# Causal maxima in a decoder kernel: two units to a turn on TensorE, scores in two strips of rows and two banks

## What is computed

```python
scores = jnp.einsum('bhqd,bhkd->bhqk', q, k) * SCALE
mask = _window_mask(N, N)
scores = jnp.where(mask[None, None], NEG_INF, scores)
attn = jax.nn.softmax(scores, axis=-1)
out = jnp.einsum('bhqk,bhkd->bhqd', attn, v)
```

## Time and profile before

| | us |
|---|---|
| three runs, median | 1609.12 |
| three runs, lowest and highest | 1601.79, 1609.81 |
| profiled execution | 1603.94 |
| its span | 1602.2 |
| PE busy | 1361.3 |
| DVE busy | 1332.5 |
| ACT busy | 1037.2 |
| mean granted clock of PE | 0.939 |

### The profile page before, as it was taken

The page is one execution under the profiler, slowest core; times in us unless marked ns, Lnnn a source line. Parts: engine busy times, 40 slices in busy tenths (PEclk is TensorE's granted clock), DMA queues, the critical chain, the costliest instruction groups (busy, mean ns, idle before and its releaser), DMA issues.

```text
span 1602.2 us, 32850 instructions
## 1 busy us (share of the span) xinstructions
PE 1361.3 (85%) x13068; PEld 745.7 (47%) x13068; DVE 1332.5 (83%) x1965; ACT 1037.2 (65%) x1884; POOL 428.2 (27%) x495
## 2 busy tenths in 40 slices
PE   3778878879899999898978767879999998999986
PEld 2454535344445453444443333446555555555643
DVE  6988989979879888887798899888788888978743
ACT  3244365465673865765695769886899788989431
POOL 1432141132240422321331240241222313122310
PEclk9697989799999999999999988889999999999988
DMA  6313122200201111002120003011020211101020
GB/s 223 93 54 93 34 68 68 74 15 1 75 15 41 36 41 42 21 22 54 63 89 28 1 1 132 20 41 44 2 71 13 59 39 33 41 5 44 2 81 27
DMA packets 54201, 76.24 MB, mean 48 GB/s; under 512 B 8480, under 2 KB 23840, under 8 KB 53536
## 3 DMA queue, kind: packets, MB, share of 16 engines
q1 hardware_dynamic: 54048, 74.14, 16.2%
HBM read 38.98 MB, written 9.44 MB: 30 GB/s over the span
## 4 chain that ended last, share of the span: by engine, by line
PE 47%; DVE 29%; ACT 10%; issue 7%; POOL 4%; DMA 1%; SPq 1%; ACTq 0%; DVEq 0%; POOLq 0%
PE bank L200 16%; DVE mix_NM L1079 4%; PE bank L1178 4%; PE bank L534 3%; DVE ssm_HS L1537 2%; PE bank L542 2%; PE bank L522 2%; PE bank L992 2%; PE bank L1204 2%; PE bank L557 2%; DVE ffn_m L1133 2%; PE bank L977 2%; POOL attn_P L737 2%; PE bank L495 1%; DVE ffn_Z L1142 1%
## 5 line engine op out<-in xcount | busy, mean ns | idle before, releaser
L1052 ACT ACTIVATE mix_P<-bank 128x512 f32<-128x512 f32 x256 | 142.3, 604 | 50.6 <-PE bank L977 50.2
L1079 DVE TENSOR_REDUCE mix_NM<-bank 128x2 f32<-128x512 f32 x256 | 162.8, 682 | 11.2 <-PE bank L952 10.4
L737 POOL TENSOR_SCALAR_AFFINE_SELECT cross_P<-cross_P 128x256 f32<-128x256 f32 x128 | 90.5, 717 | 272.9 <-ACT cross_P L642 272.4
L1296 POOL TENSOR_TENSOR ffn_room<-ffn_room 128x512 f32<-128x512 f32 x64 | 89.9, 1406 | 263.9 <-ACT ffn_room L1235 167.0
L1537 DVE TENSOR_TENSOR_SCAN ssm_HS<-ssm_DA,ssm_DD 128x1024 f32<-128x1024 f32 x64 | 150.3, 2348 | 10.1 <-ACT ssm_DD L1488 5.5
L737 POOL TENSOR_SCALAR_AFFINE_SELECT attn_P<-attn_P 128x256 f32<-128x256 f32 x128 | 89.6, 713 | 243.7 <-ACT attn_P L642 243.7
L1485 ACT ACTIVATE ssm_DA<-ssm_Z,A_T 128x255 f32<-128x255 f32 x256 | 110.9, 498 | 3.1 <-DVE ssm_HS L1537 2.7
L642 ACT ACTIVATE attn_P<-bank 128x384 f32<-128x384 f32 x128 | 63.8, 498 | 63.1 <-PE bank L523 62.7
L642 ACT ACTIVATE cross_P<-bank 128x384 f32<-128x384 f32 x128 | 62.6, 489 | 50.9 <-PE bank L523 50.5
L1543 DVE TENSOR_TENSOR ssm_HS<-ssm_HS,ssm_CS 128x1024 f32<-128x1024 f32 x64 | 82.0, 1281 | 0.9
L1460 ACT ACTIVATE ssm_Z<-bank 128x512 f32<-128x512 f32 x128 | 72.2, 599 | 13.4 <-PE bank L1374 12.8
(11 more groups left out here) (410 smaller groups left out, 4043.3 us busy)
## 6 DMA issues: line engine op xcount, KB each, us to landing
attn_stack<-attn_P SPq DMA_DIRECT2D x96, 128.0 KB, 2.4
cross_stack<-cross_P SPq DMA_DIRECT2D x96, 128.0 KB, 2.4
ffn_room<-f_gate SPq DMA_DIRECT2D x4, 1024.0 KB, 5.3
XR<-x SPq DMA_DIRECT2D x8, 512.0 KB, 6.8
ffn_room<-f_up SPq DMA_DIRECT2D x4, 1024.0 KB, 5.6
ffn_room<-f_down SPq DMA_DIRECT2D x4, 1024.0 KB, 4.9
x_mid<-XR SPq DMA_DIRECT2D x8, 512.0 KB, 3.0
XR<-x_mid SPq DMA_DIRECT2D x8, 512.0 KB, 3.7
```

Source lines behind the costliest of these rows:

```text
L737: nc.gpsimd.affine_select(out=diagonal, in_=diagonal, compare_op=ALU.is_ge, fill=0.0, base=0, pattern=[[0, 2], [1, P]], channel_multiplier ...
L1052: nc.scalar.activation(self.p[h % 8], bank[b4[h % 2]][:, :], ACT.Exp, scale=HD2 ** -0.5).then_inc(s["p_ready"], 1)
L1079: nc.vector.tensor_reduce(self.nm[:, t, 16 * i + 2 * g:16 * i + 2 * g + 2], bank[b4[u % 3]][:, :].rearrange("p (c k) -> p c k", c=2), AX.X ...
L1296: nc.gpsimd.tensor_tensor(self.inter[q % 2][:, 512 * (g % 2):512 * (g % 2) + 512], self.sg[g % 2], self.up[g % 2], ALU.mult).then_inc(s["i ...
```

## The change

The loop over units on PE goes in steps of two. One turn issues units u and u + 1 together. It takes both banks first (`banks.take` with two banks). In one part it issues the two masks, in the other the score pieces of the two units in alternation, on their two strips of rows and into their two banks. Pairs 0, 4 and 8 (named by their first unit) compute scores first, pairs 2, 6 and 10 masks first. Each unit still raises `s_ps` with its own last matmul. The pieces, their sizes and their number are the same; four of the eight later units have pieces of 128 columns, as before, now 6, 7, 10 and 11.

PE's string loses six letters for each sequence, 96 in all: the pair stands at the place of its second unit. In 65 of the 96 pairs the two units stood next to each other; in the other 31 the turns of other blocks that stood between them now stand ahead of the pair. In DVE's string one letter moves, in sequence 6 of layer 0. The strings of SP, ACT and POOL stay.

```diff
--- before.py
+++ after.py
...
     "pe": (
-        "aaaaaaaaaaaaaaaaaaaaaaaaaaaaaaaaaacacacaaaacaaaaaaaaaaaaaaaaaaaaaaaaaccaaaaaaaaaaaaabcaaaaaaabba"
...
+        "aaaaaaaaaaaaaaaaaaaaaaaaaaaacacacaaaacaaaaaaaaaaaaaaaaaaaaaaaaaccaaaaaaaaaaaaabcaaaaaaabbaaaaaaa"
...
     "dve": (
...
-        "ffddfddddddaddfddddfdddddddddddddfbbbbffbfbfbbbffdffbbbdfffbdffddfeddfffddddddfdddddfdddddfddddd"
+        "ffddfddddddaddfddddfdddddddddddddfbbbbffbfbfbbffbdffbbbdfffbdffddfeddfffddddddfdddddfdddddfddddd"
...
@@ -466,37 +465,38 @@
                     last.then_inc(self.v_ps, 1)
                     banks.read_by(b, self.v_ready, TT * n + t + 1)
 
-                for u in range(self.UNITS):
-                    yield
-                    b, j = self.b[(2 + u) % 3], u % 4
-                    rows = slice(32 * j, 32 * j + 32)
-                    q, k = self.qk[rows, Q_HIGH], self.qk[rows, K_HIGH]
+                for u in range(0, self.UNITS, 2):
+                    yield
                     if u == 0:
                         pe.wait_ge(self.qk_ready, DC * n + DC)
-                    banks.take(b)
-                    masked = u % 2 == 1
+                    two = [(w, self.b[(2 + w) % 3], slice(32 * (w % 4), 32 * (w % 4) + 32)) for w in (u, u + 1)]
+                    banks.take(*(b for _, b, _ in two))
+                    masked = u % 4 == 2
                     for part in ("mask", "scores") if masked else ("scores", "mask"):
                         begins, ends = part == ("mask" if masked else "scores"), part == ("scores" if masked else "mask")
-                        if part == "mask" and u < 4:
-                            last = nc.tensor.matmul(bank[b][:, :].rearrange("p (c k) -> p c k", c=DC), ident16[:],
-                                                    broadcast(hide_qk[:, :], 1, DC), start=begins, stop=ends)
-                        elif part == "mask":
-                            last = nc.tensor.matmul(
-                                bank[b][:, :].rearrange("p (c k) -> p c k", c=2)[:, :, P:S], ident16[:],
-                                broadcast(hide_qk[:, :], 1, 2), start=begins, stop=ends)
-                        elif u < 4:
-                            for c in range(DC):
-                                last = nc.tensor.matmul(bank[b][:, c * P:(c + 1) * P], q[:, c, 0:P], k[:, c, 0:P],
-                                                        start=(begins and c == 0), stop=(ends and c == DC - 1))
+                        if part == "mask":
+                            for w, b, _ in two:
+                                whole_bank = bank[b][:, :].rearrange("p (c k) -> p c k", c=DC if u < 4 else 2)
+                                last = nc.tensor.matmul(whole_bank if u < 4 else whole_bank[:, :, P:S], ident16[:],
+                                                        broadcast(hide_qk[:, :], 1, DC if u < 4 else 2),
+                                                        start=begins, stop=ends)
+                                if ends:
+                                    last.then_inc(self.s_ps, 1)
+                            continue
+                        if u < 4:
+                            pieces = [(c, slice(0, P), slice(0, P), c * P) for c in range(DC)]
                         else:
-                            for i in range(2):
-                                c = 2 * ((u - 4) // 4) + i
-                                for keys in (slice(0, P), slice(P, S)) if masked else (slice(0, S),):
-                                    last = nc.tensor.matmul(bank[b][:, i * S + keys.start:i * S + keys.stop], q[:, c, P:S],
-                                                            k[:, c, keys], start=(begins and i == 0),
-                                                            stop=(ends and i == 1 and keys.stop == S))
-                    last.then_inc(self.s_ps, 1)
-                    banks.read_by(b, self.s_max, self.UNITS * n + u + 1)
+                            pieces = [(2 * ((u - 4) // 4) + i, slice(P, S), keys, i * S + keys.start) for i in range(2)
+                                      for keys in ((slice(0, P), slice(P, S)) if masked else (slice(0, S),))]
+                        for i, (c, queries, keys, at) in enumerate(pieces):
+                            for w, b, rows in two:
+                                last = nc.tensor.matmul(bank[b][:, at:at + keys.stop - keys.start],
+                                                        self.qk[rows, Q_HIGH][:, c, queries], self.qk[rows, K_HIGH][:, c, keys],
+                                                        start=(begins and i == 0), stop=(ends and i == len(pieces) - 1))
+                                if ends and i == len(pieces) - 1:
+                                    last.then_inc(self.s_ps, 1)
+                    for w, b, _ in two:
+                        banks.read_by(b, self.s_max, self.UNITS * n + w + 1)
 
                 yield
                 b = self.b[2]
```

More of the change, by code:

```diff
@@ L52 @@
-        "hhhhhhhhihhihhhhhhhhhihhhhhhhhhhhhhihihihihihhhihhhhihihhhhhhhhihihhihhhhhhhhiiiiiiiiiii"),
+        "aaaaaaaaaaaaaaaaaaaaaaaaaaaacacacaaaacaaaaaaaaaaaaaaaaaaaaaaaaaccaaaaaaaaaaaaabcaaaaaaabbaaaaaaa"
+        "baabbcbaaaaaabaaaabacaabacaabaaabaababaaaaabaaabaababaaaaaabaaaabcaaaaaaaaaabaaacabaabbbabbacacb"
+        "abababaaababbaaaabababaaabbabbccbbaabbbbbbaaaaaaaabbaabbccabbabaaaababaababaababaabaabababababba"
+        "baaabaabbbbabacbabacbababaaababaaaabbacbbcabaaabbabbabbabbbabaaaaaaaabbabbccbabaaabaabadadabddba"
@@ new lines @@
+        "badbadbabdbadbdbaaabdadaabdabddabaadabbabddbbabdbdbbdddadadadbabdaddaddabbaabbababddaaddbbadbdad"
+        "abddadbababdbabbbdaaddaaddaaaabbaabbddbadbadbddbadabaddbaaaaaaabddbddbadabaabaaaaaabddbdbaabdbdd"
+        "bddaabdbaabdabbbdabbabdabbaddabbadaaabbabdabdabbaabdadbabbaaabdbabbdbaadddaadaabbaaababddabdabdd"
+        "babaaaababddabadbaabdaadbabaababdbdbdbaabaadaabdbddbaabbbddbbbdbabbbddbbabdbbabbdbbbbddbdbbadbdd"
+        "addaddadabbabbaabaddbadbadababdbadabdabdabababbadbdbababddbaaaaaabaabdbdababbdbdbbddabbdabbdabba"
@@ new lines @@
+        "abbabbbaabbbabbabbaabaaaaaaaababaabbaababadbdbdabdabdabadbdabdbdbadabaaabaaaaddbadadabaabdabddda"
+        "adbdaabaaabaaabbbddbbbbdbbbdbbbbdeebbbdbbbbbdbbbddeededdbbdbbeedbdeebeebebedebedbbdbeebeebdbdebe"
+        "ebeeebddbdbdbddddbdbdbdbbbdbbbdbbdbbdbbbdbbdbbddbbdbbdbdbbbdddddeddddedddfddddefddddfeeddfdeedee"
+        "eddeeddfeeeedddddfdddeddefeeefgeegeefgeeggfgeeegefeefhehhefhhfhhhhhehhheehhhhhffheegehghhhefhhgh"
+        "hhfhghghhghghhfhhheefheehhfehhhhhhhhehhehhhhhhhhihhhhhhhihffheiiehehfhehehehgihhhehehihhihgeehih"
@@ new lines @@
+        "gihhhghgehhegghhhehhhhheehhffhhhhhhihhheeihehhehehhhfieheeihehehehffheihehhhehehehhhihfheehiffhh"
+        "egiehgeieegehhegghhgghhhhhheffhheeehhehehhhhhihhhihehhhhffheeehehffhihiheehhhhfhfhehhhghehihhghe"
+        "hgeehheegeeghhhhgghhehehiieefhheeiihhheehhhhhihhhehhihhhffheeefhehehfhiihehehhhfhehehhhfihehhfhh"
+        "geehgeeehhgieiggeehhgghheehhhhiiehheeffhehehhhhhhihhhhfhheiheehffheeihihffhehehfhghhhehghehhhghe"
+        "hhhheehegghhiegegehhheehhhhhfeehhihhhhhhhhhehhhhhehehefeheiehehffihehfhihfhhhehfhhhhfhgihhghhigh"
@@ L53 @@
+        "gghhgghhhhhhhhihhihhhhhhhhhihhhhhhhihihihihihhhihhhhihihhhhhhhhihihhihhhhhhhhiiiiiiiiiii"),
     "act": (
```

## The result

| | before | after |
|---|---|---|
| median, us | 1606.98 | 1638.73 |
| profiled span | 1602.2 | 1636.6 |
| mean granted clock | 0.939 | 0.923 |

The change makes the kernel slower: the ratio is 1.0205, with a 95% interval of 1.018 to 1.0229. That is 32 us where 16 were forecast, and 1638.7 lies 1.7 us above the forecast range. The direction and the late hand-over came as forecast; the size did not, because a second part of the change costs about as much.

What follows compares the result with a forecast made beforehand. Neither PE nor DVE was taken to bound the kernel alone, but DVE to pace the pass with PE following. 17.3 + 3 - 2.4 - 2 gave +16 us, 1620 from 1603.94; range 1604 to 1637.

Steps and rivals of the forecast that it cites:

- DVE paces the pass, hand-over one reduction late: In each pass (a sequence's twelve units of maxima), pairs wait for both banks, so DVE idles: 1.5 us longer at full clock.
- The hand-over's sum: Growth from late pair starts over the 16 passes: 17.3 us in ten, 6 us in the other six.
- the ten passes of the chain: Passes 0, 1, 3, 8, 9 and 11 to 15, through which the chain of waits goes: 17.3 us longer.
- I make these six 6 us together: Passes 2, 4, 5, 6, 7 and 10, where reductions stand among other work: 6 us longer together, bounds 0 and 9.
- count half, 3: Of the 6 us in those six passes, 3 us were counted, since the chain is mostly elsewhere.
- The credits against it: Taken off: 2.4 us of PE switches saved in passes 4 to 7, and 2 us for PE leaving passes less late.
- The base: The sum of +16 us was added to the profiled execution of before, 1603.94 us, giving 1620.
- The clock rival: Longer passes lose the granted clock; if six more do, 11 us more, 1631; chance 0.17.
- strips that don't overlap: Interleaved score pieces of a pair would go one after the other: 12 us more, 1632; chance 0.03.

Runs made afterwards that it cites:

- e7: After's pair code in the 65 adjacent pairs only; the other 31 keep before's two turns and order, with before's tables; 1625.0 us, ratio 1.0099 to before.
- e5: After plus the fill, one added zero matmul of 512 columns in each pair that changes no value; 1633.2 us, ratio 1.0138 to before.
- e1: After's merged turns and tables, but inside a turn unit after unit as in before, each taking its own bank; 1622.7 us, ratio 1.0102 to before.
- e6: Before plus the fill (zero matmul, 512 columns) in even units, without passes 4 to 7; 1602.2 us, ratio 0.9946 to before.
- e8: Merged turns with before's order inside a pair, in layer 1 only, layer 0 as before; 1614.1 us, ratio 1.0037 to before.
- e9: Before plus the fill (zero matmul, 512 columns) in even units, without passes 0 and 3 to 7; 1601.5 us, ratio 0.9964 to before.
- e3: After, but the score pieces of a pair's two units stand one unit after the other instead of alternating; 1639.6 us, ratio 1.0201 to before.

## Why the prediction missed

- **DVE paces the pass, hand-over one reduction late.** Right, to 0.1 us. Idle before units 4 and 6 was forecast at 0.19 and 0.30 and measured at 0.19 and 0.30, before unit 2 0.51 against 0.59. At half clock 0.55 and 0.76 were worked out, and pass 0 has 0.73 before unit 6 (1.93 from pair to pair, less 1.20) and 0.52 before unit 8 (1.72):

```profile
59.15 1.29 DVE L683 TENSOR_REDUCE attn_NM<-bank 128x2 f32<-128x512 f32 x2 [0.43 <-PE bank L480]
61.08 1.29 DVE L683 TENSOR_REDUCE attn_NM<-bank 128x2 f32<-128x512 f32 x2 [0.64 <-PE bank L493]
62.80 1.29 DVE L683 TENSOR_REDUCE attn_NM<-bank 128x2 f32<-128x512 f32 x2 [0.43 <-PE bank L480]
```

- **The hand-over's sum.** The passes were to grow by 17.3 + 6 = 23.3 and grew by 26.3. The prediction had 17.3 for the hand-over in the ten passes of the chain; e7, which has it without the moved turns, measured 17.5. This part was sized right. By single passes it was less exact: the four that were to be 1.5 longer each at full clock (8, 9, 11, 12) are 1.8 to 2.7 longer in after, since the clock fell in them, and 1.5 to 1.7 in e5.
- **The moved turns: the step that failed.** "I make these six 6 us together" and "count half, 3" was what stood for passes with moved turns, and no term at all stood for what the blocks behind a late unit lose. e1 measured 15.4. I had looked at the moved turns for DVE idle time inside the pass only. Of the 20.5 us by which e1's profiled span is longer, 7.4 lie inside the passes (pass 7 alone 2.8) and 13 between them; the medians differ by 15.4, so some 5 of these 13 are chance of which execution was profiled.
- **The credits against it.** I took off 2.4 for saved switches and 2 for PE leaving earlier. No run measures either. In e7 the span grew by 0.5 less than the passes did, so there is no sign of more than that.
- **The base.** The sum was added to the profiled 1603.94, but the median of before is 1606.98. Of the 19 us between 1620 and 1638.7, 3 come from this.
- **The clock rival.** The clock fell as this rival has it: passes 8, 9, 11 and 12 went to between 0.69 and 0.90. By the mean clock, 0.061 x 1602 = 98 us of full-speed time was withheld before and 0.077 x 1637 = 126 after. The price of 11 us is not borne out: the fill shows some 4 us in the five passes that DVE paces, and over the whole kernel it gives before nearly as much as after. The Trainium skill, TensorE: Matmul & The Clock Gate, section Why this matters for your kernels, warns against an idle TensorE between bursts of matmuls. e5 and e6 agree in direction, with 0.945 against 0.923 and 0.948 against 0.939; the waits here are short ones, of 0.24 to 0.78 us in pass 12 of after.
- **The range.** It ended at 1637 because its slowest cases were a colder clock and strips that don't overlap; none had the moved turns at more than 6. With 15 in place of 3 the sum would have been 28 instead of 16.

Not settled: where between the passes e1 loses its time, and through which waits, so that the moved turns are located as a cause but not explained (single profiled executions don't tell: in e8, which has before's order in all of layer 0, pass 1 starts 4.6 us later than in before); whether the DVE letter matters; whether a pair at the first unit's place would do in layer 0, where DVE's list as it stands would have to change with it.

## What to carry to other kernels

With k buffers in turn, a producer that takes two at once works with k - 1: price the hand-over from the end of the consumer's step that frees the second buffer, and compare it with what the consumer still has in hand. When merging moves a step behind another block's work, ask which in-order list wants that step next, and price every moved step, between the edited stretches as well as in them. Where an engine waits for another anyway, time saved on it buys little; but work without use that keeps TensorE's clock at full can pay, as in e6 and e9. And when a remedy helps the changed kernel, try it on the kernel before too: only the difference belongs to the change.

## What was not expected of the hardware

- Score pieces on two strips of 32 rows overlap as well when they stand four behind four as when they alternate: e3 and after take the same time, and pass 12 of after has eight pieces in 0.40 us, with 0.41 for eight of two units before.
- One useless matmul of 512 columns a pair (in pass 9 of e6 the next one starts 0.23 us after it) kept the granted clock at 1.00 to the end of pass 15, where it was 0.53 before and 0.50 after, and made the kernel before 0.5% faster. It did not in pass 0, where e6 has 0.50.
